# Layer-normalised x turned in a ring of four and started inside the weight fold; the experts' row roots moved behind the low half of y

## The reference

```
h = concat(tokenizer(x), txt)                       # 8 x 640 x 192
xn = layernorm(h)
k, v = xn @ Wk, xn @ Wv                             # 12 heads of 64
q    = ln(gelu(xn @ Wq[g] @ Wt[g] + bt[g])) * gt + betat      # 4 groups g
kf, qf = phi(k), phi(q) / sqrt(128)                 # phi(x) = [relu(x), relu(-x)]
kv, ksum = kf^T v, sum over tokens of kf
out  = qf kv / (qf ksum + 1e-6)
h   += gelu(ln(out @ Wf + bf)) @ Wo + bo
h   += soft_experts(layernorm(h))                   # l2-normalised rows and slots, two softmaxes
```

## Time and profile before

| what | us |
|---|---|
| median of three runs (2393.21 to 2393.94) | 2393.47 |
| the profiled execution, its own time | 2393.88 |
| its span, from first to last instruction | 2392.2 |
| tokenizer | 0 to 470.6 |
| weight fold | 470.6 to 502.0 |
| keys and values | 502.0 to 705.1 |
| attention | 705.4 to 2331.8 |
| soft experts | 2332.1 to 2392.2 |

### The profile page before, as it was taken

The page is one execution under the profiler, slowest core; times in us unless marked ns, Lnnn a source line. Parts: engine busy times, 40 slices in busy tenths (PEclk is TensorE's granted clock), DMA queues, the critical chain, the costliest instruction groups (busy, mean ns, idle before and its releaser), DMA issues. The chain is left out here.

```text
span 2392.2 us, 58381 instructions
## 1 busy us (share of the span) xinstructions
PE 2260.3 (94%) x20906; PEld 1549.3 (65%) x20906; DVE 2006.3 (84%) x3025; ACT 1841.5 (77%) x2852; POOL 1282.6 (54%) x1250
## 2 busy tenths in 40 slices
PE   5999999979988999999999999999999999999965
PEld 3677677656655666666666666666666666666644
DVE  6999999878868888888888888888888888888835
ACT  6677676567668888888888888888888888888834
POOL 0000000056667767676767776767777777676750
PEclk9999999989999999999999999999999999999987
DMA  6412211123322222222222222222222222222212
GB/s 148 133 41 51 48 39 39 24 77 94 89 75 41 43 44 42 44 45 43 44 44 42 44 42 44 42 44 42 44 42 44 42 44 43 46 42 44 42 22 67
DMA packets 319407, 123.72 MB, mean 52 GB/s; under 512 B 298164, under 2 KB 309940, under 8 KB 319028
## 3 DMA queue, kind: packets, MB, share of 16 engines
q1 hardware_dynamic: 318196, 122.44, 24.2%
q10 hardware_dynamic: 1152, 0.51, 0.1%
HBM read 41.62 MB, written 9.18 MB: 21 GB/s over the span
## 5 line engine op out<-in xcount | busy, mean ns | idle before, releaser
L1108 ACT ACTIVATE phi<-ps_t,betat,gt 64x512 f32<-64x512 f32 (+1 forms) x1280 | 850.7, 665 | 17.3 <-PE ps_t L1007 0.2
L1039 PE MATMUL ps_y<-staging,o_turned 128*128 128x384 bf16 x3840 | 821.2, 326 | 0.0
L1321 POOL TENSOR_TENSOR phi_lo<-phi 128x512 bf16<-128x512 f32 x480 | 505.2, 1053 | 439.6 <-ACT phi L1108 439.6
L1039 PEld LDWEIGHTS ps_y<-staging,o_turned 128*128 128x128 bf16 x3840 | 362.1, 98 | 219.1 <-issue 0.8
L1039 PE MATMUL ps_y<-wf_lo,o_turned 128*128 128x384 bf16 x1920 | 469.5, 326 | 0.0
L1313 POOL TENSOR_TENSOR q_ssq<-q_ssq,half 128x8 f32<-128x8 f32 x240 | 418.2, 1743 | 18.8
L172 PE MATMUL acc<-w_b,feat 128*128 128x384 bf16 x1728 | 295.8, 331 | 34.5 <-ACT feat L223 28.0
L1196 DVE TENSOR_TENSOR o_halves<-o,o_halves 128x512 bf16<-128x512 f32 x240 | 191.3, 797 | 157.9 <-ACT o_halves L1118 157.8
L1098 ACT ACTIVATE shared<-shared 128x512 f32<-128x512 f32 x240 | 150.1, 625 | 177.3 <-DVE shared L1159 176.9
L1039 PEld LDWEIGHTS ps_y<-wf_lo,o_turned 128*128 128x128 bf16 x1920 | 188.0, 98 | 124.7 <-issue 0.7
L172 PEld LDWEIGHTS acc<-w_b,feat 128*128 128x128 bf16 x1728 | 168.5, 99 | 150.6 <-DVE w_b L298 23.2
(11 more groups left out here) (256 smaller groups left out, 4684.4 us busy)
## 6 DMA issues: line engine op xcount, KB each, us to landing
xt<-in_x_dram SPq DMA_DIRECT2D x32, 320.0 KB, 5.3
ex_big<-in_wf_dram SPq DMA_DIRECT2D x24, 384.0 KB, 3.4
xt<-in_x_dram SPq DMA_DIRECT2D x32, 256.0 KB, 5.7
x_kept<-x_halves SPq DMA_DIRECT2D x40, 128.0 KB, 2.0
o_turned<-o_halves SPq DMA_TRANSPOSE x240, 3.1
out_dram<-h SPq DMA_DIRECT2D x8, 480.0 KB, 4.9
staging<-in_wq_t_dram SPq DMA_DIRECT2D x1, 3072.0 KB, 12.3
staging<-in_tok_w_dram SPq DMA_DIRECT2D x8, 240.0 KB, 10.4
```

The lines of the kernel that those rows point to most:

```text
L1039: last = nc.tensor.matmul(ps_y[:, n, 0:HC], lhs, w[part][:, c, n * HC:(n + 1) * HC], start=c == 0 and lhs is hi and part == 'wf_hi', stop= ...
L1108: last = nc.scalar.activation(phi[sign * DH:(sign + 1) * DH, j % 2, a:b, head, :], ps_t[rows, a * P:b * P].rearrange("p (i n) -> p i n", n ...
L1321: nc.gpsimd.tensor_tensor(phi_lo[:, j % 2, :, head], phi[:, j % 2, :, head], phi_hi[:, j % 2, :, head], ALU.subtract).then_inc(s["phi_lo_d ...
```

## The change

What it does:

- **Key inputs.** A class `KeyInputs` holds xn, the halves (`xs`, two buffers, now 3·128 columns and no column of ones) and the turned x (`xt`, four buffers used as the ring 0 1 2 0 1 2 0 1 2 3, was two). The high half is one ACT instruction over 192 columns, was two. Halves and turns of tiles 0, 1, 2 are made in the fold, at u = 17 to 20; SP waits for all three turns before the fold's barrier.
- **Order on SP in `keys_and_values`.** For tile n SP now issues the store of tile n + 1, then the turn of tile n + 3, then, in tiles t = 1 and t = 4, the loads of Wf. The turn of tile n + 3 waits for the low half of tile n + 3 (`x.low` at n + 4).
- **x_kept.** The stored tensor is the turned x (3·128 columns), so `load_x` in `attend` is two plain DMAs instead of one transposing one; the fourth piece of x with the rows of ones is set once by POOL.
- **Experts.** POOL does `low_ys` before `row_roots` in slot 0 of tile 40; the power for the slots' norms is split off (`slot_roots`) into slot 4, behind `rstd_y`; DVE makes `row_factors` in slot 2, was slot 5.

The core of the diff:

```diff
+class KeyInputs:
+    LEAD = 3
+    RING = (0, 1, 2, 0, 1, 2, 0, 1, 2, 3)
+    def high_half(self, x):
+        self.nc.scalar.activation(self.xs[:, x, 0:DIM], self.xn[:, :], ACT.Copy).then_inc(self.high, 1)
+    def turn(self, sp, n):
+        at, _ = self.place(n // self.PERIOD, n % self.PERIOD)
+        sp.dma_start(self.xt[:, at], self.xs[:, n % 2, :], transpose=True).then_inc(self.turned[at], 16)
 # attention_weights: SP
+                for n in range(x.LEAD):
+                    sp.wait_ge(x.low, n + 1)
+                    x.turn(sp, n)
+                for n in range(x.LEAD):
+                    sp.wait_ge(x.turned[n], 16)
 # attention_weights: ACT, after q_hi of step u (FIRST = 17)
+                    if FIRST <= u < FIRST + x.LEAD:
+                        n = u - FIRST
+                        act.wait_ge(x.norm, n + 1)
+                        if n >= 2:
+                            act.wait_ge(x.turned[n - 2], 16)
+                        x.high_half(n % 2)
 # attention_weights: DVE, after q_lo of step u
+                    if FIRST < u <= FIRST + x.LEAD:
+                        n = u - FIRST - 1
+                        dve.wait_ge(x.high, n + 1)
+                        x.low_half(n % 2)
+                    if FIRST <= u < FIRST + x.LEAD:
+                        n = u - FIRST
+                        ...
+                        x.normalize(h, stats, n)
 # keys_and_values: SP
                 def turn_x(n):
-                    sp.wait_ge(xl_ready, n + 1)
-                    if n >= 2:
-                        sp.wait_ge(projected, 2 * n - 2)
-                    sp.dma_start(xt[:, n % 2], xs[:, n % 2, 0:3 * P], transpose=True).then_inc(turned[n % 2], 16)
-                    sp.dma_start(x_kept[n], xs[:, n % 2, :]).then_inc(kept[n % 2], 16)
+                    sp.wait_ge(x.low, n + 1)
+                    last = max((m for m in range(n) if x.RING[m % x.PERIOD] == x.RING[n % x.PERIOD]), default=None)
+                    if last is not None:
+                        sp.wait_ge(projected, 2 * last + 2)
+                        sp.wait_ge(x.kept, 16 * (last + 1))
+                    x.turn(sp, n)
...
                 load(0)
                 load(1)
-                for n in range(2):
-                    turn_x(n)
+                keep_x(0)
                 for n in range(TILES):
                     b, t = divmod(n, TPB)
-                    if n + 2 < TILES:
-                        turn_x(n + 2)
+                    if n + 1 < TILES:
+                        keep_x(n + 1)
+                    if n + x.LEAD < TILES:
+                        turn_x(n + x.LEAD)
                     if t == 1:
                         load(PER_BATCH * b + 2)
 # attend: SP
-                    sp.dma_start(x[:, :, :], x_kept[t], transpose=True).then_inc(s["x_in"], 16)
+                    kept = x_kept[t].rearrange("p (k n) -> p k n", k=3)
+                    sp.dma_start(x[:, 0:3], kept).then_inc(s["x_in"], 16)
+                    sp.dma_start(x[0:TAIL, 3], kept[0:TAIL, 1]).then_inc(s["x_in"], 16)
 # attend: DVE
+                    if j == 2 and not tile.real and prev.real:
+                        dve.wait_ge(s["ex_root"], 2)
+                        row_factors(nc, dve, ex, slice(0, KEPT), s["ex_steps"], 2)
                     if j == 5 and not tile.real and prev.real:
                         dve.wait_ge(s["ex_root"], 3)
-                        row_factors(nc, dve, ex, slice(0, KEPT), s["ex_steps"], 2)
                         slots_scale()
 # attend: POOL
-                    if j == 0 and not tile.real and tile.prev().real:
-                        row_roots()
                     if j == 4 and tile.prev().real:
                         rstd_y(tile.prev())
                     if j == 0 and tile.prev().prev().real:
                         low_ys(tile.prev().prev())
+                    if j == 0 and not tile.real and tile.prev().real:
+                        row_roots()
+                    if j == 4 and not tile.real and tile.prev().real:
+                        slot_roots()
```

More of the change, by code:

```diff
@@ L498, in keys_and_values @@
         ps_kv = ctx.enter_context(nc.psum_tensor("ps_kv", [P, 2, 2, 512], F32))
-        ones_set, x_norm, xh_ready, xl_ready = (sem(n) for n in ("ones_set", "x_norm", "xh_ready", "xl_ready"))
-        turned, kept = ([sem(f"x_{name}{n}") for n in range(2)] for name in ("turned", "kept"))
+        ones_set = sem("ones_set")
         projected, kf_ready, kpos_lo_ready, kneg_lo_ready, v_hi_ready, v_lo_ready = (sem(n) for n in (
@@ L558, in _ @@
                             load(PER_BATCH * (b + 1) + k)
-                for k in range(2):
-                    sp.wait_ge(kept[k], 16 * TILES // 2)
+                sp.wait_ge(x.kept, 16 * TILES)
             @block.tensor
@@ L565, in project @@
                     n = TPB * number(b) + t
-                    x, uses = halved(b, t)
+                    at, uses = place(b, t)
                     if hf == 0:
-                        pe.wait_ge(turned[x], 16 * uses + 16)
+                        pe.wait_ge(x.turned[at], 16 * uses + 16)
                     if not early:
@@ L612, in high_x @@
                 def high_x(b, t):
[L613 to L621, removed]
+                    act.wait_ge(x.norm, TPB * number(b) + t + 1)
+                    at, uses = place(b, t - 2)
+                    act.wait_ge(x.turned[at], 16 * uses + 16)
+                    x.high_half(parity(b, t))
                 def key_features(n, t, hf, early):
@@ L648, in batch @@
                         key_features(n, t, 1, first)
-                        if not (last and t >= TPB - 3):
-                            high_x(of, t + 3)
+                        if not (last and t >= TPB - x.LEAD):
+                            high_x(of, t + x.LEAD)
                         if t < PER_BATCH:
@@ L654, in batch @@
                                                  ACT.Copy).then_inc(wf_hi_ready, 1)
-                act.wait_ge(ones_set, 12)
-                for t in range(3):
-                    high_x(0, t)
+                act.wait_ge(ones_set, 8)
                 all_batches(act, batch)
@@ L665, in normalize @@
                 def normalize(n):
[L666 to L669, removed]
+                    dve.wait_ge(x.low, n)
+                    x.normalize(h, stats, n)
                 def low_x(b, t):
[L672 to L675, removed]
-                                            ALU.subtract).then_inc(xl_ready, 1)
+                    dve.wait_ge(x.high, TPB * number(b) + t + 1)
+                    x.low_half(parity(b, t))
                 def halves(n, t, hf, early):
@@ L704, in batch @@
                         halves(n, t, 1, first)
-                        if not (last and t >= TPB - 3):
-                            low_x(of, t + 3)
-                        if not (last and t >= TPB - 4):
-                            normalize(n + 4)
+                        if not (last and t >= TPB - x.LEAD):
+                            low_x(of, t + x.LEAD)
+                        if not (last and t >= TPB - x.LEAD - 1):
+                            normalize(n + x.LEAD + 1)
                 for t_, v in ((v_hi, 1.0), (v_lo, 0.0)):
@@ L990, in queries @@
                     if j == 0:
-                        pe.wait_ge(s["x_in"], 16 * count(tile, 0, 1))
+                        pe.wait_ge(s["x_in"], 32 * count(tile, 0, 1))
+                        pe.wait_ge(s["x_ones"], 3)
                     free_bank(pe, use_tile, f"oct{j}")
```

98 lines of the change are left out of this document (64 added, 34 removed).

## The result

The changed kernel takes 2397.99 us (median of 15 runs, 2396.47 to 2404.36), the kernel before in the same session 2393.72 (15 runs, 2391.14 to 2396.39). The ratio is 1.0022, 95% interval 1.0014 to 1.0029: slower by about 0.2%. 2385.4 was predicted, in a range of 2378.5 to 2391.5. The profiled execution of the changed kernel took 2402.28 us (span 2400.6), 4.3 above its median.

A forecast was written before the change was run, and what follows sets the result against it. PE was taken to set the time in the key stage and the attention. The terms −13.6 − 1.3 + 6.6 + 0.2 = −8.1 us, from a median of 2393.47, gave 2385.4 us, range 2378.5 to 2391.5.

The forecast's parts named there:

- Tail, −13.6: End of the attention: PE's 11.72 us gap and the half clock after it go, move_y slips 1.1; −13.6 us.
- Fold and first tile, −1.3: Weight fold and first projection: PE starts at 505.9 instead of 507.25, as turns are made in the fold; −1.3 us.
- Loads of Wf, +6.6: Key stage: loads queued behind SP's new wait come late, stall ACT and partly reach PE; +6.6 us, bounds −3 and +29.
- The step that failed: Key stage: PE's v_lo waits cover about 1.5 us more of tile 2's lateness, leaving 7 × 0.6 + 8 × 0.3.
- the 0.7: Key stage: ACT idles 59.3 us over 80 halves, 0.7 each, taken to cover 0.7 us of each stall.
- a late low half makes the next load later still: Key stage: one lateness feeds the next; an argument for the loads being paid nearly in full, without its own size.
- x in the attention, +0.2: Attention: two plain loads replace a turning one; PE waits for the second only at the start; +0.2, to +1.5 us.
- Paid nearly in full: Rival, key stage: late loads cost some 18 us since PE needs both POOL and ACT; 2396.8 us, chance 0.12.
- Hidden: Rival, key stage: shorter landings or larger ACT slack hide the late loads; 2378.8 us, down to 2376, chance 0.17.
- the forecast that rested on both covers: Key stage +2 to +12 us, with ACT's idle time and PE's v_lo waits as covers: 2380.8 to 2390.8, chance 0.65.
- The bound of +29: Key stage: upper bound if each late load is paid in full, 7 × 1.3 + 8 × 2.5 us.

The follow-up runs named there:

- run 1: Changed kernel with SP issuing all loads of Wf ahead of the turn of tile n + 3: 2379.71 us, ratio 0.9944 to the kernel before.
- run 9: run 1 with POOL making both pieces of Wf's low half behind both kf_lo of a tile: 2371.25 us, ratio 0.991.
- run 6: Changed kernel with only the fifth tile's (t == 4) loads of Wf ahead of the turn, the second tile's load staying behind: 2389.93 us, ratio 0.997.
- run 7: Changed kernel with only the second tile's (t == 1) load of Wf ahead of the turn, the fifth tile's staying behind: 2387.61 us, ratio 0.9962.
- run 4: Changed kernel, loads still late, with POOL making both pieces of Wf's low half behind both kf_lo of a tile: 2389.49 us, ratio 0.9981.
- run 5: Kernel before with the next batch's two loads of Wf issued one tile later (t == 4 becomes t == 0): 2427.34 us, ratio 1.0129.
- 16 in tile 0: Kernel before with sixteen short ACT copies ahead of the first copy of Wf in each batch: 2399.1 us, ratio 1.0023.
- 16 in tile 2: Kernel before with sixteen short ACT copies ahead of the third copy of Wf in each batch: 2398.55 us, ratio 1.0018.
- 8 in tile 0: Kernel before with eight short ACT copies ahead of the first copy of Wf in each batch: 2390.6 us, ratio 0.9986.
- run 2: Kernel before with the tail's edits alone (low half of y first, norms' power in slot 4, row_factors in slot 2): 2380.05 us, ratio 0.9944.

## Why the prediction was wrong

**What one late copy costs.** For each run, from the first projection until 2222 of the stage's 2240 products have run: ACT's waits or delays and their places, PE's idle time over that of its base (the kernel before 15.3; run 1 14.7; run 9 9.6), and what is left per place.

| kernel | ACT late, us (places) | PE idle, base | hidden per place | PE busy, clock |
|---|---|---|---|---|
| changed | 23.1 (13) | 28.9, 14.7 | 0.7 | 186.5, 0.96 |
| run 6, tile 2 late | 17.6 (8) | 22.4, 14.7 | 1.2 | 180.7, 0.99 |
| run 7, tile 0 late | 10.1 (7) | 16.8, 14.7 | 1.1 | 180.6, 0.98 |
| run 4, POOL's order | 28.8 (15) | 24.1, 9.6 | 1.0 | 182.3, 0.98 |
| run 5, a tile later | 26.0 (7) | 33.5, 15.3 | 1.1 | 194.2, 0.92 |
| 16 in tile 0 | 12.2 (8) | 19.4, 15.3 | 1.0 | 182.5, 0.98 |
| 16 in tile 2 | 12.2 (8) | 19.5, 15.3 | 1.0 | 181.2, 0.99 |
| 8 in tile 0 | 6.1 (8) | 13.6, 15.3 | 1.0 | 178.9, 0.99 |

About 1 us of each lateness is hidden, in either tile, and the rest is idle time of PE. Where the waits are longest, PE's busy time grows as well (180.7, at 0.99, in the kernel before). The rows of runs 6 and 7 are of their shortest executions.

**Point by point.**

- *Tail, −13.6.* Right: −13.3 in the profile, −13.8 alone (run 2). Clock 1.00, no gap, row_factors directly ahead of move_y. Even its parts hold: on the scale of before PE's last fuse ends at 2304.6, 14.7 earlier as written, and move_y is held 1.4 by row_factors (1.1 were written).
- *Fold and first tile, −1.3.* Right in its place: the first projection starts at 505.65, was 507.25. In whole times it can't be told from nothing: run 1, with it, equals run 2, without it.
- *Loads of Wf, +6.6.* Wrong; the profile has +19.5, and the medians of runs with and without late loads 18 to 19. The mechanism was there, and ACT's lateness was if anything overstated: 29.1 us in 15 places by the prediction, 23.1 in 13 measured. Tile 0 had 1.2 to 3.0, 11.8 in all (1.3 each, 9.1 in all were written); tile 2 had 11.3 in six of eight batches (2.5 each, 20 in all).
- *The step that failed* is "behind which ACT has spare time: about 1.5 more for the second kind. So 7 × 0.6 + 8 × 0.3". The waits for v_lo were taken as a cover for the copy in tile 2. They are none there: sixteen short copies in tile 2 cost as much as in tile 0, and the waits stay beside the new ones (11.5 us). It is a delay in tile 0 that takes them off (0.8 left, with 15.9 for kf_lo instead), so they are part of the 1 us hidden in that tile, to which the prediction had not put them. With the 0.7 alone the step would have read 7 × 0.6 + 8 × 1.8 = 18.6, and the sum 2397.4; 2398.0 was measured.
- *A term that was missing* is the clock: no line had PE slow down in the key stage. Of +19.5, 5.9 are busy time at 0.96, and only 13.6 idle. In slices of 25 us the kernel before has a clock below 1.00 in the first alone, the changed one in five of nine, 0.90 to 0.93. The prediction counted half clock only where it ended, in the tail. So 18.6 would have hit partly for the wrong reason: it is made of waiting alone, and of what was measured only 13.6 is. That the sum would have met the median within 0.6 us is luck also in that the lateness it starts from, 29.1, was 23.1.
- *The two kinds are not independent.* 6 and 4 us alone, 18 to 19 together (runs 6, 7). The prediction named this, "a late low half makes the next load later still", as an argument for a rival and gave it no price.
- *x in the attention, +0.2.* The small load is no trouble: 16 KB land in 2.0 us, 96 KB in 1.9, where the turning load took 2.6.

```profile
shared<-x_kept SPq DMA_DIRECT2D x40, 96.0 KB, 1.9
shared<-x_kept SPq DMA_DIRECT2D x40, 16.0 KB, 2.0
```

The Trainium skill (DMA: Bandwidth & Descriptors, Specifications) has transfers below 512 B short of line rate. By that the second load is the poor one: a sixth of the bytes for the same time fits it, or a fixed cost; these rows don't part the two. Either way nobody waits for it in the middle of the attention.

- *The rivals.* "Paid nearly in full" with 2396.8 is what happened, and it had 0.12. "Hidden" had 0.17, and 0.65 went to the forecast that rested on both covers. The bound of +29 was in the text; the range did not reach to it.

**What stays open.** Why late transfers cost more than equal work: 26.0 us of waiting for loads in 7 places (run 5) took 31 us, 12.2 us of short copies in 8 took 6. The table explains most of it by 1 us hidden per place and 13.5 us of clock; that longer pauses of PE bring the lower clock is a reading of the two traces, not tested by a run of its own. Nor is it settled how the cost divides in the changed kernel between POOL's kf_lo and ACT's key features: PE's waits name POOL there, but with POOL out of the way most of the cost stays (runs 4 and 9).

## What to carry to other kernels

When a statement is moved behind a new wait on a queue, everything behind it in that queue moves too; price the loads behind it, and look first whether they can simply stand ahead of it. A wait in the trace counts as cover only for the place and the engine at which it stands: a delay of known length, set in by short instructions, measures the cover of a place in one run, and here it said 1 us in both places tried. In a stage where PE is busy 92% of the time (181.4 of 197.9 us) a pause may have a second price, a lower clock behind it; no run here tests that by itself. And before an 8 us gain is taken as proof of a mechanism, make the same edit where the mechanism is absent.

## What the runs showed of the hardware that was not expected

- A small delay of ACT made the kernel no slower but slightly faster (eight short copies a batch, 0.9986), and GpSimd's order alone brought 8 us on top of run 1. In both, DVE's subtractions of kf_lo get shorter: a mean of 821 ns before, 756 with eight short copies; 809 in run 1 and 723 in run 9, at the same size. v_lo stays at 550. Where GpSimd stands still beside DVE's kf_lo, a single one takes 0.54 to 0.56 us in the kernel before; where GpSimd works all the while, 0.55 to 1.27. That the gains come from where the two meet is not shown: the changed kernel is slower and has the shortest mean of all, 706 ns, and with eight short copies PE's busy time is 1.7 us less than before as well. DVE's groups in run 1, then in run 9, from 508 to 695 us:

```profile
L738 DVE TENSOR_TENSOR kf_lo<-kf 128x384 bf16<-128x384 f32 x77 | 62.3, 809 | 28.9 <-ACT kf L692 28.6
```

```profile
L738 DVE TENSOR_TENSOR kf_lo<-kf 128x384 bf16<-128x384 f32 x80 | 57.8, 723 | 35.3 <-ACT kf L692 34.6
```

- Sixteen ACT copies of 128x4 elements take 1.62 us from start to end, 0.1 each, though a single one is recorded with 0.2.
- The granted clock over the key stage is lowest where PE's pauses are many and long: 0.99 with 15.3 us of PE idle time, 0.96 with 28.9, 0.92 with 33.5 in fewer and longer pieces (up to 4.4 us). Below that the order is not strict: 0.98 with 16.8 and with 24.1, 0.99 with 22.4.
